# Gated cross-attention: softmax numerators divided before they are split into pairs

## The reference

```python
scale = DIM_HEAD ** (-0.5)
q = (x @ W_q).reshape(b, n, HEADS, DIM_HEAD)
k = (context @ W_k).reshape(b, j, HEADS, DIM_HEAD)
v = (context @ W_v).reshape(b, j, HEADS, DIM_HEAD)
sim = jnp.einsum('bihd,bjhd->bhij', q, k) * scale
sim = jnp.where(mask[:, None, None, :], sim, max_neg)
attn = jax.nn.softmax(sim, axis=-1)
out = jnp.einsum('bhij,bjhd->bihd', attn, v).reshape(b, n, INNER)
return out @ W_o + b_o
...
h = bitlinear(x, w1, b1)       # bitlinear: rmsnorm, rows to 8 bits, weights to -1, 0, 1
h = jax.nn.gelu(h, approximate=False)
return bitlinear(h, w2, b2)
...
x = x + jnp.tanh(g_xattn[0]) * _L0_xattn_ref(_layernorm(x, axis=-1), ctx_768, ...)
x = x + jnp.tanh(g_ffn[0]) * _L0_ffn_ref(_layernorm(x, axis=-1), ...)
```

## Time and profile before

| | us |
|---|---|
| runs | 1071.88, 1072.07, 1073.18 (median 1072.07) |
| the profiled execution | 1070.9 |
| its span, first to last instruction | 1069.1 |
| clock of TensorE over the span | 0.99 of full speed |
| DMA queues, share of the 16 engines | 80.5% |

### The profile page before, as it was taken

How to read it: one execution, slowest core, us unless ns; L and a number is a source line. 1 busy time by engine, 2 the same in 40 slices (tenths; PEclk the granted TensorE clock), 3 DMA queues, 4 the chain that set the end, 5 groups by cost and what they waited for, 6 DMA issues and landing times. The chain is left out here.

```text
span 1069.1 us, 26540 instructions
## 1 busy us (share of the span) xinstructions
PE 995.9 (93%) x9856; PEld 579.5 (54%) x9856; DVE 835.2 (78%) x1707; ACT 805.7 (75%) x1374; POOL 712.1 (67%) x691
## 2 busy tenths in 40 slices
PE   3988899999999999999999998999999999999877
PEld 2455565565555655555556555556565565555443
DVE  4788798778798777777779876788878776886976
ACT  3976787977878668796868867697786977777766
POOL 5577998577676776567576575767668666956651
PEclk9999999999999999999999999999999999999989
DMA  7989999787879979697877986988867889868750
GB/s 225 280 163 228 206 170 174 133 184 128 163 142 180 174 116 192 115 167 162 157 129 126 200 163 130 183 143 139 177 128 158 175 162 171 167 110 139 148 96 30
DMA packets 472335, 169.17 MB, mean 158 GB/s; under 512 B 450320, under 2 KB 452368, under 8 KB 471824
## 3 DMA queue, kind: packets, MB, share of 16 engines
q1 hardware_dynamic: 472208, 167.48, 80.5%
HBM read 48.28 MB, written 7.34 MB: 52 GB/s over the span
## 5 line engine op out<-in xcount | busy, mean ns | idle before, releaser
L1339 POOL TENSOR_TENSOR p<-prob,p 128x750 f16<-128x750 f32 x224 | 358.5, 1614 | 110.4 <-ACT p L1189 108.1
L1007 DVE CUSTOM_DVE_ANT_0 prob<-ps_s,mbias 128x750 f32<-128x750 f32 x224 | 204.0, 933 | 58.8 <-PE ps_s L820 47.1
L1182 ACT ACTIVATE prob<-prob,rmin 128x750 f32<-128x750 f32 x224 | 204.3, 914 | 26.2 <-DVE rmin L1007 25.8
L787 PE MATMUL ps_g<-ctx,wk 128*128 128x375 f16 x1152 | 201.8, 327 | 23.4 <-POOL ctx L1350 16.4
L787 PE MATMUL ps_g<-wv,ctx 128*128 128x512 f16 (+1 forms) x864 | 197.0, 379 | 4.1 <-DVE k_sb L1026 2.2
L787 PEld LDWEIGHTS ps_g<-ctx,wk 128*128 128x128 f16 x1152 | 111.2, 99 | 105.6 <-issue 25.7
L820 PE MATMUL ps_s<-k_sb,q_sb 64*32 64x375 f16 (+2 forms) x2688 | 128.8, 322 | 15.6 <-DVE rmin L1007 15.4
L787 PEld LDWEIGHTS ps_g<-wv,ctx 128*128 128x128 f16 (+1 forms) x864 | 86.8, 103 | 101.0 <-issue 5.9
L849 PE MATMUL ps_g<-pt,v_sb 128*64 128x224 f16 (+2 forms) x2448 | 122.8, 254 | 2.6 <-DMA pt<-p 2.4
L1189 ACT ACTIVATE p<-prob 128x750 f16<-128x750 f32 x144 | 116.0, 820 | 3.5 <-DMA pt<-p 3.0
L849 PEld LDWEIGHTS ps_g<-pt,v_sb 128*64 128x64 f16 x2448 | 109.6, 110 | 2.9 <-issue 2.8
(11 more groups left out here) (134 smaller groups left out, 1524.6 us busy)
## 6 DMA issues: line engine op xcount, KB each, us to landing
ctx_f<-in_ctx SPq DMA_DIRECT2D x47, 375.0 KB, 4.0
xa<-in_x SPq DMA_DIRECT2D x16, 448.0 KB, 4.7
xr<-in_x SPq DMA_DIRECT2D x28, 256.0 KB, 3.4
out<-xr SPq DMA_DIRECT2D x28, 256.0 KB, 2.8
pt<-p SPq DMA_TRANSPOSE x254, 4.0
h_sb<-in_w SPq DMA_DIRECT2D x4, 512.0 KB, 4.6
w<-in_w SPq DMA_DIRECT2D x3, 512.0 KB, 5.0
xr<-in_w SPq DMA_DIRECT2D x3, 512.0 KB, 5.4
```

The costliest lines, as they stand in the source:

```text
L787: mm = nc.tensor.matmul(out, lhs, rhs, start=(m == 0), stop=(m == len(steps) - 1))
L1007: nc.vector.tensor_tensor_reduce(prob[:, (b * NU + n) % PROBS, :].rearrange("p (c k) -> p c k", c=2), ps_s[:, n % 2, :, 0:CH], mbias[:, :] ...
L1182: nc.scalar.activation(prob[:, (b * NU + n) % PROBS, :], prob[:, (b * NU + n) % PROBS, :], ACT.Exp, bias=rmin[:, n:n + 1], scale=-1.0, acc ...
L1339: nc.gpsimd.tensor_tensor(p16[:, u % HILO, 1, 0:J], prob[:, (b * NU + n) % PROBS, :], p16[:, u % HILO, 0, 0:J], ALU.subtract).then_inc(s[" ...
```

## The change

R now takes the two units of a score group: one reciprocal of two values, and then each value by itself is multiplied by 512 (RS), in fp32. H is ScalarE's for all 14 units, and its rounding multiplies by that factor, so it waits for R (recips), which waits for the exponentials of both units. L has two forms. In units 4 and 11 VectorE makes the low half in one step from prob, the factor and the high half; in the other 12 GpSimd first multiplies prob in place (a new step, semaphore normed) and then subtracts. Whoever waited for p_lo (T on SyncE, M on VectorE) now waits for one of two semaphores, lo_dve or lo_pool, by need_lo.

PV on TensorE has its attention matmuls only. The bank is emptied by ScalarE, which rounds (PL) with the factor 1/512, and VectorE, which subtracts (PA), both from the bank; att and GpSimd's part of PL are gone. The output projection waits for attn_lo, which VectorE now gives.

All five tables are written anew; of them the diff shows the first line of VectorE's.

```diff
-    N1:0:0 XN:0:0 PW:0:0 XH:0:0 XH:1:0 PW:1:0 KL:0:0 KL:1:0 KL:2:0 KL:3:0 QL:0:0 M:0:0 M:1:0 QL:1:0 PW:2:0 M:2:0
+    N1:0:0 XN:0:0 XH:0:0 XH:1:0 PW:0:0 PW:1:0 KL:0:0 KL:1:0 KL:2:0 PW:2:0 KL:3:0 QL:0:0 QL:1:0 M:0:0 M:1:0 M:2:0
...
-    "O": ("x2", 1), "V": ("v_lo", 1), "F1": ("h_lin", NF), "PV": ("attn_raw", 1), "Q": ("q_lo", 1),
+    "O": ("x2", 1), "V": ("v_lo", 1), "F1": ("h_lin", NF), "PV": ("attn_lo", 2), "Q": ("q_lo", 1),
-def recips_units(b, n):
...
-    return slice(2 * n, 2 * n + 2) if b == LB else slice(4 * n, min(4 * n + 4, NU))
...
-def recips_for(b, n):
...
-    last = 2 * units_of(b, n)[-1] + 1
-    return last // 2 if b == LB else last // 4
...
-    return name, b * PER_BATCH[name] + n + 1
...
-HI_ON_ACT = [n for n in range(NU) if n not in (2, 5, 7, 10, 12)]
-HI_ON_POOL = [n for n in range(NU) if n not in HI_ON_ACT]
+    return name, b * PER_BATCH[name] + times * (n + 1)
...
+LO_ON_DVE = (4, 11)
+LO_ON_POOL = [n for n in range(NU) if n not in LO_ON_DVE]
...
-        rrec16 = sb("rrec16", [128, 2, NU], F16)
...
-        att = sb("att", [128, TQ], F32)
...
-        def need_hi(eng, b, n):
...
-            on_act = n in HI_ON_ACT
-            of = HI_ON_ACT if on_act else HI_ON_POOL
-            eng.wait_ge(hi_act if on_act else hi_pool, b * len(of) + of.index(n) + 1)
+        def need_lo(eng, b, n):
...
+            b, n = b + n // NU, n % NU
+            on_dve = n in LO_ON_DVE
+            of = LO_ON_DVE if on_dve else LO_ON_POOL
+            if b >= 0:
+                eng.wait_ge(lo_dve if on_dve else lo_pool, b * len(of) + of.index(n) + 1)
...
                 elif kind == "T":
...
-                    need(sp, "p_lo", b, n)
+                    need_lo(sp, b, n)
...
                 elif kind == "PV":
...
-                    need(pe, "recips", b, recips_for(b, n))
-                    j, first_query, size, row = weighs(b, n)
-                    for m in units_of(b, n):
-                        for of, q, at, many in pieces_of(b, m):
-                            if of != j or not first_query <= q < first_query + size:
-                                continue
-                            to = 256 + q - first_query
-                            for a in range(2):
-                                for e in range(2):
-                                    u = 2 * m + e
-                                    nc.tensor.matmul(g[e * DH:(e + 1) * DH, to:to + many],
-                                                     rrec16[:, a, u:u + 1].to_broadcast([128, DH]),
-                                                     ident[:, at:at + many], start=(a == 0), stop=(a == 1))
+                    j, _, size, row = weighs(b, n)
...
-            def take_reciprocals(b, n):
...
-                of = recips_units(b, n)
-                need(dve, "expd", b, of.stop - 1)
-                last = pieces_of(b - 1, (of.stop - 1) // 2)[-1][0] if b > 0 else 0
-                need(dve, "weighted", b - 1, last)
-                nc.vector.reciprocal(rrec[:, of], rsum[:, of]).then_inc(s["recips_raw"], 1)
-                need(dve, "recips_raw", b, n)
-                nc.vector.tensor_scalar(rrec16[:, 0, of], rrec[:, of], RS, None, ALU.mult)\
-                    .then_inc(s["recips_hi"], 1)
-                need(dve, "recips_hi", b, n)
-                nc.vector.scalar_tensor_tensor(out=rrec16[:, 1, of], in0=rrec[:, of], scalar=RS,
-                                               in1=rrec16[:, 0, of], op0=ALU.mult, op1=ALU.subtract)\
-                    .then_inc(s["recips"], 1)
+            def take_reciprocals(b, m):
...
+                need(dve, "expd", b, 2 * m + 1)
+                need_lo(dve, b - 1, 2 * m + 1)
+                nc.vector.reciprocal(rrec[:, 2 * m:2 * m + 2], rsum[:, 2 * m:2 * m + 2]).then_inc(s["recips_raw"], 1)
+                need(dve, "recips_raw", b, m)
+                for u in (2 * m, 2 * m + 1):
+                    nc.vector.tensor_scalar(rrec[:, u:u + 1], rrec[:, u:u + 1], RS, None, ALU.mult)\
+                        .then_inc(s["recips"], 1)
...
-                    need(dve, "p_lo", b, n - PROBS)
+                    need_lo(dve, b, n - PROBS)
...
                 elif kind == "R":
...
+                elif kind == "L" and n in LO_ON_DVE:
+                    u = b * NU + n
+                    need(dve, "p_hi", b, n)
+                    nc.vector.scalar_tensor_tensor(out=p16[:, u % HILO, 1, 0:J], in0=prob[:, u % PROBS, :],
+                                                   scalar=rrec[:, n:n + 1], in1=p16[:, u % HILO, 0, 0:J],
+                                                   op0=ALU.mult, op1=ALU.subtract).then_inc(lo_dve, 1)
                 elif kind == "PA":
-                    need(dve, "recips_out", b, n)
-                    qs = slice(0, queries_of(b, n))
-                    nc.vector.tensor_tensor(att[:, qs], g[:, qs], att[:, qs], ALU.mult)\
-                        .then_inc(s["attn_raw"], 1)
+                    pieces = attn_pieces(b, n)
+                    need(dve, "attn_hi", b, 2 * n + 1)
+                    for at, to, size in pieces:
+                        nc.vector.scalar_tensor_tensor(out=attn[:, 1, n % NP, to:to + size], in0=g[:, at:at + size],
+                                                       scalar=1.0 / RS, in1=attn[:, 0, n % NP, to:to + size],
+                                                       op0=ALU.mult, op1=ALU.subtract)\
+                            .then_inc(s["attn_lo"], 2 // len(pieces))
...
-                g = bank(kind, n, b) if kind in EMPTIED else None
+                filled = {"PL": "PV"}.get(kind, kind)
+                g = bank(filled, n, b) if filled in EMPTIED else None
...
-                elif kind == "H" and n in HI_ON_ACT:
+                elif kind == "H":
...
-                    need(act, "expd", b, n)
+                    need(act, "recips", b, n)
...
-                    nc.scalar.activation(p16[:, u % HILO, 0, 0:J], prob[:, (b * NU + n) % PROBS, :], ACT.Copy)\
-                        .then_inc(hi_act, 1)
-                elif kind == "PV":
+                    nc.scalar.activation(p16[:, u % HILO, 0, 0:J], prob[:, (b * NU + n) % PROBS, :], ACT.Copy,
+                                         scale=rrec[:, n:n + 1]).then_inc(s["p_hi"], 1)
+                elif kind == "PL":
...
-                    need(act, "attn_lo", b, 2 * n - 1)
-                    nc.scalar.activation(att[:, 0:queries_of(b, n)], g[:, 256:256 + queries_of(b, n)], ACT.Copy, scale=1.0 / RS)\
-                        .then_inc(s["recips_out"], 1)
-                elif kind == "PL":
-                    need(act, "attn_raw", b, n)
...
-                        nc.scalar.activation(attn[:, 0, n % NP, to:to + size], att[:, at:at + size], ACT.Copy)\
-                            .then_inc(s["attn_hi"], 2 // len(pieces))
+                        nc.scalar.activation(attn[:, 0, n % NP, to:to + size], g[:, at:at + size], ACT.Copy,
+                                             scale=1.0 / RS).then_inc(s["attn_hi"], 2 // len(pieces))
...
-                if kind == "H" and n in HI_ON_POOL:
+                if kind == "L" and n in LO_ON_POOL:
...
-                    need(pool, "expd", b, n)
-                    need_turned(pool, u - HILO)
-                    nc.gpsimd.tensor_copy(p16[:, u % HILO, 0, 0:J], prob[:, (b * NU + n) % PROBS, :]).then_inc(hi_pool, 1)
-                elif kind == "L":
...
-                    u = b * NU + n
-                    need_hi(pool, b, n)
-                    nc.gpsimd.tensor_tensor(p16[:, u % HILO, 1, 0:J], prob[:, (b * NU + n) % PROBS, :],
-                                            p16[:, u % HILO, 0, 0:J], ALU.subtract).then_inc(s["p_lo"], 1)
-                elif kind == "PL":
-                    pieces = attn_pieces(b, n)
-                    for m, (at, to, size) in enumerate(pieces):
-                        need(pool, "attn_hi", b, 2 * n + (1 if m == len(pieces) - 1 else 0))
-                        nc.gpsimd.tensor_tensor(attn[:, 1, n % NP, to:to + size], att[:, at:at + size],
-                                                attn[:, 0, n % NP, to:to + size], ALU.subtract)\
-                            .then_inc(s["attn_lo"], 2 // len(pieces))
+                    held = prob[:, u % PROBS, :]
+                    need(pool, "p_hi", b, n)
+                    nc.gpsimd.tensor_scalar(held, held, rrec[:, n:n + 1], None, ALU.mult).then_inc(s["normed"], 1)
+                    pool.wait_ge(s["normed"], b * len(LO_ON_POOL) + LO_ON_POOL.index(n) + 1)
+                    nc.gpsimd.tensor_tensor(p16[:, u % HILO, 1, 0:J], held, p16[:, u % HILO, 0, 0:J], ALU.subtract)\
+                        .then_inc(lo_pool, 1)
...
```

479 lines of the change are left out of this document (236 added, 243 removed).

## The result

The changed kernel takes 1184.78 us (1183.16 to 1185.10, 4 runs), the kernel before beside it 1071.97 (1071.46 to 1073.18): a ratio of 1.1047 [1.1028, 1.1067] (in brackets the 95% interval, here and below). It is slower by 10.5%, where 1058.5 was forecast. The profiled execution has a span of 1183.1 us, 114 more than before.

What follows compares the result with a forecast made beforehand. TensorE was taken as the bound, 97% of the time in the middle. The terms -15 - 2.4 - 2.2 + 4 + 2 = -13.6 us on the median of 1072.07 gave 1058.5 us, with 1047 to 1074 for 8 in 10.

Steps and rivals of the forecast that it cites:

- The step that failed: GpSimd's 192 new in-place multiplications of numerators: 0.833 us each, 160 us, 192 with delays; GpSimd's total -5 to +27 on 712.
- it has the room: GpSimd can take added work, since it waited 110 us before L1339 and 61 before L1345.
- TensorE: 640 small matmuls that spread the reciprocals removed, 22 to 25 ns each: -15 us; waits for the reciprocals go too, -2.4.
- The -2.2 for the tail: Output projection no longer waits for GpSimd's step on the way out of the attention bank: -2.2 us.
- ScalarE: Busy time: 68 copies gone, 80 roundings at 0.820 us new; net +43 us, from 805.7 to about 848.
- VectorE: Busy time: old steps out (-110.6), reciprocals, scalings, bank subtractions and lower halves in; net +33 us, from 835 to 868.
- The waits in the middle: TensorE's waits after the head: extra load +14 us by a queueing estimate, wider-spaced score groups -10; taken as +4.
- rival (a): New order gains more than load costs: middle waits fall by 10, head costs nothing; 1043 to 1050 us, chance 0.14.
- The head: TensorE's first matmuls start later, at 18 to 19 us, since GpSimd makes the layer norm's scale first: +2 us.
- (b): VectorE and GpSimd get in each other's way, VectorE's lower halves take 3 us: 1066 to 1085 us, chance 0.14.
- (c): ScalarE becomes the bound as its rounding H waits for VectorE's reciprocal R: about 1072 or above 1075, chance 0.15.
- (d): Removed small matmuls (L837) only filled time in which TensorE awaited transposes; small, in the range, no chance of its own.

Runs made afterwards that it cites:

- two_op: The changed kernel with a second, neutral operation (times 1.0) in GpSimd's in-place multiplication: 1047.44 us, 0.9758 of the kernel before.
- slow_three: two_op with the one-operation multiplication back in three of GpSimd's twelve units (0, 5, 9): 1072.11 us, 1.0006 of the kernel before.
- two_op_spread: two_op with the 640 small spreading matmuls put back on constant data, nobody waiting for them: 1057.11 us, 0.9843 of the kernel before.
- imm_one_op: The changed kernel with immediate 1.0 for the per-partition factor in GpSimd's multiplication (still one operation) and ScalarE's rounding: 1169.36 us, one run.
- slow_six: two_op with the one-operation multiplication back in six of GpSimd's twelve units (0, 2, 5, 7, 9, 12): 1099.9 us, one run.
- two_op_head: two_op with the order of the kernel before at the start on GpSimd, VectorE, ScalarE and SyncE: 1044.92 us, 0.9748 of the kernel before.

## Why the prediction was wrong, point by point

**The step that failed** is GpSimd's: "The nearest row is the mask's L1357, 750 columns, median 0.833 us ... 160 us; at 1.0 us with delays 192". L1357 multiplies and adds in one instruction, the new step only multiplies. It measured 2.171 us (median), 432 us in all, and GpSimd rose by 273 instead of -5 to +27. All five tensor_scalar lines of GpSimd in the kernel before have two operations, so the cost of one was unknown. A row nearer to the new step than the mask's was among them, in place, fp32, with a factor per partition:

```profile
L1323 POOL TENSOR_SCALAR xr<-xr,winv x3: 1116/1116/1123, 75.9 to 132.4; 128x1024 f32<-128x1024 f32 x3
```

By columns it gives 0.82 to 0.87 us for 750, near two_op's 0.898: operands and types were not what was wrong, the number of operations was. The prediction did not ask for it, and my upper end was the taken value plus some delay, not a far row. Even L1339's 1.614 us would have given 310 us, and GpSimd above 850. A rival in which GpSimd becomes the bound was missing altogether.

**Beside it, "it has the room"** was wrong as well. GpSimd's idle 110 and 61 us were no reserve: 60 us more than two_op has cost 25 (slow_three).

**TensorE.** -15 forecast, -9.7 measured (two_op_spread). The mechanism was right, the size too large by what fell into waits. The 2.4 us for the reciprocals went. The -2.2 for the tail did not show. The wait for GpSimd's attention half is gone there (0.2 us for VectorE's in two_op's tail; over the whole run 2.2 us in 3 pieces, at most 1.7), but TensorE is free for 21.4 of two_op's last 84.1 us and for 16.3 of those of the kernel before, and two_op has a wait of 5.9 us for ScalarE (L1243) in it.

**ScalarE.** 848 forecast, 864.6 measured. The rounding was priced by L1189 at 0.820, but it now has a factor per partition and takes 0.911; imm_one_op without it takes 0.821. 224 x 0.091 = 20 us covers the miss of 16.6. The Trainium skill (ScalarE: Activation LUTs, section What ACT_TABLE_LOAD costs) gives about 93 ns for each per-partition operand; the trace agrees, and I had not used it.

**VectorE.** 868 forecast, 823.1 measured. Each single scaling takes 0.149, not 0.214 (L1137 has two operations), and the two of a pair overlap: 24.1 us busy in all, not 47.9. The lower half takes 1.275 us instead of 1.5 on average, 0.99 undisturbed, -7 us; the 96 bank subtractions 0.307 for 0.30, the 112 reciprocals 0.158 for 0.164, together -3. The sum had also left the other steps as they were; of these the split of x fell from 42.0 to 30.7 us:

```profile
L979 DVE SCALAR_TENSOR_TENSOR p<-prob,rrec,p 128x750 f16<-128x750 f32 x32 | 40.8, 1275 | 2.9 <-ACT p L1162 2.8
L986 DVE SCALAR_TENSOR_TENSOR attn<-ps_g,attn 128x224 f16<-128x224 f32 (+6 forms) x96 | 26.5, 307 | 20.1 <-ACT attn L1169 20.1
L915 DVE TENSOR_SCALAR rrec<-rrec 128x1 f32<-128x1 f32 x224 | 24.1, 149 | 3.9
L912 DVE RECIPROCAL rrec<-rsum 128x2 f32<-128x2 f32 x112 | 17.6, 158 | 16.2 <-ACT prob L1155 15.9
```

**The waits in the middle.** +4 was taken between -10 and +14. With the cheap form, TensorE is busy in 832.3 of the 851 us (822.7 before), and over the whole run its waits for the score exits are 10.4 us (7.0 in two_op_spread), not 15.4: the lower end was the nearer, rival (a)'s mechanism. In that stretch VectorE (694 for 672 us), ScalarE (723 for 660) and GpSimd (629 for 582) are all busier than before, and TensorE waits less, so the queueing estimate had the wrong sign. two_op, the changed kernel with the cheap form, is 25.7 us better than before, where 13.6 was forecast. Without the 9.7 and the 2.4 us above and with the head's 1.1 to 2.5, an estimate of -15 to -16 us is left for the middle and the tail, below even the lower end of -10. So two_op's 1047.44, at the edge of the range of 1047 to 1074, doesn't confirm the sum: this term was too high by more than the others were too low.

**The head.** +2 forecast, TensorE's start at 18 to 19 us. It started at 19.8 us in the changed kernel and at 19.5 in two_op, 3.1 later than before. The time lost is 1.1 us by the ratios and 2.5 by the medians, neither clear of the noise: that the start comes later was right, its price is not shown.

**Rivals.** (b) GpSimd and VectorE in each other's way: VectorE's lower half has a median of 0.999 and a most of 2.37 us in the changed kernel; all 32 together took 41 us, less than in the forecast (in two_op, with the faster GpSimd, the median is 1.280 and the sum 44.7), and the split of x, with a median of 1.183 us before, now has 0.750. It is not the cause. (c) H waiting for R: 35.2 us in the changed kernel and 16.5 in two_op, under the 60 named; not the cause. (d) some of it: 5 of 15 us. The other sign of being wrong did show: TensorE's waits for banks of K, V and Q grew from 15.0 to 36.5 us, by more than the 15 named. It came from GpSimd: in two_op they are 3.7.

## What to carry to other kernels

Price an instruction by a row of the same engine with the same number of operations, the same operand kinds and the same types; where there is none, take the far rows as bounds and give the case in which that engine becomes the bound its own chance. On GpSimd write an elementwise step on a tensor and a scalar with two operations, the second neutral, and look at the trace for steps with one. Idle time of an engine in a ring of buffers is no reserve: ask what each of its steps releases. After moving a step, look for the place where its queue and its neighbour's no longer fit.

## What was not expected of the hardware

- GpSimd's tensor_scalar with one operation takes 2.10 us for 750 columns, with two 0.83, and a copy 0.81; for one operation 2.53 ns a column, for two 0.84. VectorE shows nothing like it: its subtraction with one operation takes 0.486 us at least for 512 columns (L1045), and a single value takes 0.149 us with one operation and 0.214 with two.
- A factor per partition instead of an immediate costs 0.07 us on GpSimd (0.898 against 0.832, 2.171 against 2.097) and 0.09 on ScalarE.
- TensorE's own work grew as it waited more: the same 9216 matmuls are 1015.5 us busy in the changed kernel and 978.4 in two_op. The granted clock was 0.86 of full speed (2.4 GHz) between 50 and 134 us, where TensorE was busy in 64 of 84 us, and 0.96 in two_op, where it was busy in 74. In the stretch behind it is 0.97 against 1.00. Clock and busy time don't go strictly together: in the same 84 us imm_one_op has 0.90 with 63 us busy, slow_six 0.92 with 70, and two_op_head 0.94 with 74. How much of these 37 us lies in the 137 between the two kernels, and that the lower clock follows from the waits, is not shown; no run here tested it.
